# Last attention chunk: softmax reciprocals on turned sums and the output projection tile by tile; first eight MLP tiles transposed before the quantisation scale is known

## The chip, the cores and the metric

The kernel runs on one core of one Trainium2 chip. The metric is the device time of one execution in microseconds (us), as the median of several runs. TensorE is PE in the profile (PEld is its weight load), VectorE is DVE, ScalarE is ACT, GpSimd is POOL, SyncE, which issues most DMAs, is SP (SPq in rows on its queue).

## The reference, cut to what matters

```python
def reference(x, ctx_1024, g_xattn, g_ffn, Wq, bq, Wk, bk, Wv, bv, Wo, bo, w1, b1, w2, b2):
    # x: (2, 2048, 512), ctx_1024: (2, 77, 512), 16 heads of 32, hidden width 2048
    x = x + tanh(g_xattn[0]) * attention(layernorm(x), ctx_1024, ctx_1024, ...)   # softmax over 77 keys
    x = x + tanh(g_ffn[0]) * ffn(layernorm(x))
    return x

def _quant_per_tensor(x):
    scale = max(max(abs(x)), 1e-6) / 127.0        # one scale for the whole tensor
    return round(x / scale), scale

def ffn(x):
    h = qlinear(x, w1, b1)                        # quantised x and w1, product times both scales
    return qlinear(gelu(h, approximate=False), w2, b2)
```

The scale of the first quantised product needs the largest absolute value of the whole normalised tensor, so nothing can be rounded for the MLP before the last token of the attention is done.

## The kernel before, in words

The 4096 tokens are 8 chunks of 512 (`NC`), each 4 tiles of 128 (`TT`). PSUM has 8 banks of 128x512 f32. The program has three blocks with a barrier of all engines between them: `attention`, `hidden` (first MLP product and GELU) and `output` (second product). Each engine's instructions are written out by hand, and semaphores tie the engines together; there is no scheduler.

**attention**: a step for each chunk, in a pipeline two chunks deep. `values` and `sums` (L477, L487) multiply the exponentials with V and with a pattern of ones, so that bank `BS` holds the softmax sums: partition 32r+j holds the sum of head 4j+r for j below 4 (group j, place r), the token is the column. For a chunk, `reciprocals` (DVE, L937) inverts the whole bank of 128x512, and `divide` (DVE) does for each of four groups of heads a shuffle that spreads the group's rows over 32 partitions (L930) and a product (L932). `c_high` (ACT, L721) and `c_low` (POOL, L1174) split the result in two parts for a product of f32 precision in three terms, so that `project_out` (PE, L503) has 12 matmuls for each tile. `residual` (DVE, L944) adds to the residual stream `x1`; `stats2`/`tail_stats` and `tail_mean` (L951, L966, L973), ACT's centring (L727, L823) and `amax2`/`tail_amax` (L960, L978) give mean, variance and largest absolute value; POOL's `rstd_2` (L1154) gives the reciprocal standard deviation.

The last step (`last_steps` of every engine) does this for chunk 7, whose projection (L628) goes first through the head groups 0 and 1 for all four tiles and then tile by tile through groups 2 and 3. 36 idle transposes of the identity (`idle_turns`, L60) follow it on PE. Chunks 0 and 1 (tiles 0 to 7) have been normalised in place by POOL two steps earlier.

**hidden**: DVE reduces the maxima, PE turns them (L1437), DVE makes the scale (L1515 to L1520). Then tiles 0 to 7 are prepared: DVE scales each and adds a magic number that rounds (`y`, L1532), PE transposes the result (`magic_words`, L1394), ACT or DVE subtracts the magic number and writes bf16 into `xq_t` (L1467, L1525). `half` (L1405) is a half of one of the first three products of the first pair of chunks. Each `m` of a pair of chunks is 8 matmuls (L1421), a GELU on ACT (L1493) into a ring of four tiles `h_ring`, a maximum on DVE (L1582) and a DMA of 512 KB to memory on SP (L1355), which the GELU four places on waits for:

```python
                            act.wait_ge(h_out[m % RING], 16 * ((MF // RING) * j + m // RING))
```

Tiles from 8 on are normalised by DVE (`normalized`, `round_tile`, L1553 and L1562) beside the products. On SP the block begins with two loads on the same queue as all its stores:

```python
                sp.dma_start(w2_raw[:, :, :], w2_t.rearrange("(m p) d -> p m d", p=P)).then_inc(w2_in, 16)
                sp.dma_start(sh.b2[:], b2.rearrange("(o d) -> o d", o=1).to_broadcast([P, D])).then_inc(b2_in, 16)
```

Of the kernel before, what the change touches and what calls it, by code (L numbers as in the profile page):

```python
# [22 lines left out]
P = 128  # L23
# [103 lines left out]
def attention(nc, sem, sh, x, x_t, ctx_t, wq_t, wk_t, wv_t, wo_t, bq, bk, bv, bo, w1_t, b1, g_xattn, g_ffn,  # L127
# [8 lines left out]
    with ExitStack() as own:  # L136
# [46 lines left out]
        wq_mean = rsum_g  # L183

# [66 lines left out]
        rsum_on = sem("rsum_on")  # L251
        shuf_on = sem("shuf_on")
# [35 lines left out]
        def row_bank(n):  # L288

            return BS if n == 1 else BC  # L290

# [12 lines left out]
        with nc.Block() as block:  # L304
# [69 lines left out]
            def _(pe):  # L374
# [116 lines left out]

                def project_out(c, t, begin, end):
# [118 lines left out]
                def last_steps():  # L611
                    values(LAST, GROUPS - 1)
                    sums(LAST, GROUPS - 1)
                    project_out(LAST - 1, 1, 6, ALL)
                    pe.wait_ge(x1_on, TT * (LAST - 1) + 1)
                    project_out(LAST - 1, 2, 0, ALL)
                    pe.wait_ge(c_on, GROUPS * NC)
                    project_out(LAST - 1, 3, 0, ALL)

                    hi, lo = c_parts(LAST)  # L620
                    pe.wait_ge(exp_on, PAIRS * NC)
                    first_half = [(k, t) for k in range(KD // 2) for t in range(TT)]
                    second_half = [(k, t) for t in range(TT) for k in range(KD // 2, KD)]
                    for k, t in first_half + second_half:
                        if t == 0:
                            pe.wait_ge(c_lo_on, GROUPS * LAST + k + 1)
                        for a, w in ((hi, wo_hi), (hi, wo_lo), (lo, wo_hi)):
                            mm = nc.tensor.matmul(ps[:, t, :], a[:, k, t * P:(t + 1) * P], w[:, k, :],  # L628
                                                  start=(k == 0 and a is hi and w is wo_hi),
                                                  stop=(k == KD - 1 and a is lo))  # L630
                        if k == KD - 1:
                            mm.then_inc(o_mm, 1)
                    idle_turns(nc, sh, BS, 36)
# [17 lines left out]
            def _(act):  # L651
# [54 lines left out]
                def c_copy(c, g):  # L706
# [6 lines left out]
                    nc.scalar.copy(c_sb[:, g, :], ps[:, BC, :]).then_inc(c_on, 1)  # L713

# [128 lines left out]
            def _(dve):  # L843
# [230 lines left out]
                def last_steps():  # L1074
                    reciprocals(LAST)
                    divide(LAST, 0)
                    residual(LAST - 1, 1)
                    divide(LAST, 1)
                    divide(LAST, 2)
                    residual(LAST - 1, 2)  # L1080
                    divide(LAST, 3)
                    residual(LAST - 1, 3)
                    for t in range(1, TT):
                        stats2(LAST - 1, t)
                    for t in range(1, TT):
                        amax2(LAST - 1, t)
                    for t in range(TT + 3):
                        if t < TT:
                            residual(LAST, t)
                        if 0 <= t - 1 < TT:  # L1090
                            tail_stats(t - 1)
                        if 0 <= t - 2 < TT:
                            tail_mean(t - 2)
                        if 0 <= t - 3:
                            tail_amax(t - 3)
# [178 lines left out]
def hidden(nc, sem, sh, w2_t, b2):  # L1274
# [13 lines left out]
    with ExitStack() as own:  # L1288
# [27 lines left out]
        words_act = sem("words_act")  # L1316
        words_dve = sem("words_dve")
# [8 lines left out]
        T0, T1, TX, TW = 4, 5, 6, 7  # L1326
# [4 lines left out]
        WORD_BANKS = (T0, T1, 1, 3, TW)  # L1331
        BY_DVE = (1, 3, 6)

        def words_copied(u):

            by_dve = sum(v <= u for v in BY_DVE)
            return (words_dve, by_dve) if u in BY_DVE else (words_act, u + 1 - by_dve)

        def words(u):
            return ps[:, WORD_BANKS[u % len(WORD_BANKS)], :].rearrange("p (k n) -> p k n", k=KD)  # L1340

        def first_bank(m):

            return TX if m == 2 else 2 * (m % 2)

        with nc.Block() as block:
# [29 lines left out]
            def _(pe):  # L1376
                def transposes(n, u):

                    pe.wait_ge(xq_on, n - PT + 1)
                    if not isinstance(n, int) or n >= PT + 2:  # L1380
                        pe.wait_ge(xqt_on, n - PT - 1)
# [6 lines left out]
                def magic_words(u):  # L1388

                    pe.wait_ge(y_on, u + 1)  # L1390
                    if u >= len(WORD_BANKS):
                        pe.wait_ge(*words_copied(u - len(WORD_BANKS)))
                    for k in range(KD):
                        mm = nc.tensor.transpose(ps[:, WORD_BANKS[u % len(WORD_BANKS)], k * P:(k + 1) * P],  # L1394
                                                 y[:, u % YS, k * P:(k + 1) * P], sh.ident[:])
                    mm.then_inc(xqt_mm, 1)

                def half(m, s):

                    pe.wait_ge(words_act, (PT if s else TT) - sum(u < (PT if s else TT) for u in BY_DVE))  # L1400
# [436 lines left out]
```

## Time and profile before

| | |
|---|---|
| median of 3 runs | 607.31 us (606.14 to 607.54) |
| profiled execution | 604.76 us, span 603.0 us, mean granted clock 0.994 |
| PE busy | 578.5 us (96%) |
| DVE busy | 465.3 us (77%) |
| ACT busy | 335.3 us (56%) |
| POOL busy | 246.6 us (41%) |
| attention block / hidden / output | to 355.8 / 355.8 to 486.3 / from 486.3 us |

Times in rows are microseconds from the start of the span. In a timeline row the first number is the start, the second how long the piece took, `x4` how many instructions are merged in it, and the bracket how long the engine had been idle before it and who released it. Matmuls overlap in the pipeline, so that their pitch (start to start) is less than the duration of one. A row of windows gives the granted TensorE clock as a share of 2.4 GHz.

### The profile page before, as it was taken

Reading aid. Unit: us, or ns where it says so; the run is one execution under the profiler, and the core shown is the slowest. Engines: PE = TensorE matmul, PEld = TensorE weight load, DVE = VectorE, ACT = ScalarE, POOL = GpSimd, SP = SyncE. Lnnn points to the kernel's source line nnn. Section 1 sums busy time; section 2 is a strip of 40 time slices with the busy share of each in tenths; the row PEclk is TensorE's granted clock in tenths of the full one; section 3 lists DMA queues with packets and bytes.
Section 4 is the critical chain, followed back from the end, with each engine's and each line's share of the span. In section 5 each row is a group of like instructions: output and inputs, shape, how many; then the busy total and the mean of one; then the engine's idle time right before and its main releaser. Section 6 shows DMA issues by size and latency. Waiting matters only on the chain. (4 is left out here: it accounts for less than half of the span.)

```text
span 603.0 us, 9328 instructions
## 1 busy us (share of the span) xinstructions
PE 578.5 (96%) x3340; PEld 333.1 (55%) x3340; DVE 465.3 (77%) x667; ACT 335.3 (56%) x406; POOL 246.6 (41%) x211
## 2 busy tenths in 40 slices
PE   6999899999998999999999979999999999999997
PEld 5853656657466466585665765444444454444443
DVE  5865997868869779686796887989998689955281
ACT  1556273573753836628246326777776678544440
POOL 3368366464651664916072410000003619223383
PEclk8999999999999999999999989999999999999999
DMA  9926010320411404102001149777777967799766
GB/s 305 400 92 194 33 51 6 104 107 1 176 35 38 174 0 149 63 21 86 0 1 71 71 174 357 287 280 281 278 268 289 424 234 283 265 363 366 248 221 209
DMA packets 41223, 105.57 MB, mean 175 GB/s; under 512 B 3168, under 2 KB 3936, under 8 KB 36576
## 3 DMA queue, kind: packets, MB, share of 16 engines
q1 hardware_dynamic: 39840, 103.70, 46.7%
q10 hardware_dynamic: 1344, 1.37, 0.8%
q8 instruction: 23, 0.38, 0.2%
q14 instruction: 16, 0.13, 0.1%
HBM read 63.11 MB, written 41.94 MB: 174 GB/s over the span
## 5 line engine op out<-in xcount | busy, mean ns | idle before, releaser
L1421 PE MATMUL ps<-h_sb,w_q 128*128 (+1 forms) x488 | 109.6, 379 | 0.5 <-ACT xo L1493 0.5
L1714 PE MATMUL ps<-w_q,h_q 128*128 128x512 bf16 x448 | 96.9, 379 | 0.0
L1797 POOL TENSOR_TENSOR xo<-xo,b2s 128x512 f32<-128x512 f32 x32 | 52.7, 1680 | 69.1 <-DMA xo<-x_dram 51.0
L1421 PEld LDWEIGHTS ps<-h_sb,w_q 128*128 128x128 bf16 x488 | 46.6, 98 | 52.7 <-ACT xo L1493 1.1
L1714 PEld LDWEIGHTS ps<-w_q,h_q 128*128 128x128 bf16 x448 | 43.7, 98 | 53.0
L1493 ACT ACTIVATE xo<-ps,b1s,sc 128x1024 f32<-128x1024 f32 x48 | 57.6, 1204 | 21.1 <-PE ps L1421 17.7
L689 ACT ACTIVATE q_hi<-ps,bq_sb 128x512 fp32r<-128x512 f32 x32 | 22.0, 688 | 83.5 <-DVE ps L904 77.4
L703 ACT ACTIVATE prob<-ps 77x1024 f32<-77x1024 f32 x64 | 61.6, 1013 | 12.2 <-PE ps L464 12.2
L1582 DVE TENSOR_REDUCE hmax<-xo 128x1024 f32 (+1 forms) x48 | 57.0, 1212 | 4.4 <-ACT xo L1493 4.4
L1144 POOL TENSOR_TENSOR xt_lo<-xr,xt_hi 128x512 fp32r<-128x512 f32 x28 | 35.8, 1298 | 54.8 <-ACT xt_hi L682 54.6
L1774 DVE SCALAR_TENSOR_TENSOR xo<-ps,hs,xo 128x512 f32<-128x512 f32 x32 | 23.3, 746 | 39.9 <-POOL xo L1797 38.7
L420 PE MATMUL ps<-xt_hi,wq_hi 128*128 128x512 f32 x128 | 52.4, 410 | 0.7 <-POOL xt_lo L1144 0.7
L1174 POOL TENSOR_TENSOR c_lo<-c_sb,c_hi 128x512 fp32r<-128x512 f32 x28 | 38.8, 1407 | 32.0 <-ACT c_hi L721 32.0
L1611 POOL TENSOR_SCALAR h_sb<-h_sb,sc 128x2048 f32<-128x2048 f32 x4 | 7.9, 1974 | 104.9 <-DVE sc L1590 104.9
L420 PE MATMUL ps<-xt_lo,wq_hi 128*128 128x512 f32 x128 | 50.6, 395 | 0.0
L420 PE MATMUL ps<-xt_hi,wq_lo 128*128 128x512 f32 x128 | 50.5, 395 | 0.0
L922 DVE TENSOR_REDUCE neg_max<-ps 128x16 f32<-128x1232 f32 x32 | 45.9, 1434 | 4.5 <-PE ps L431 4.4
L503 PE MATMUL ps<-wo_hi,c_hi 128*128 128x512 f32 x112 | 47.0, 420 | 0.5 <-DVE q_lo L908 0.5
L503 PE MATMUL ps<-wo_hi,c_lo 128*128 128x512 f32 x112 | 44.8, 400 | 0.0
L503 PE MATMUL ps<-wo_lo,c_hi 128*128 128x512 f32 x112 | 44.2, 395 | 0.0
L960 DVE TENSOR_REDUCE amax<-cen 128x1 f32<-128x512 f32 x28 | 19.0, 678 | 29.5 <-ACT cen L727 29.5
L1191 POOL TENSOR_TENSOR x<-x,bo_gate 128x512 f32<-128x512 f32 x32 | 40.4, 1298 | 0.0
(174 smaller groups left out, 1119.1 us busy)
## 6 DMA issues: line engine op xcount, KB each, us to landing
h_dram<-xo SPq DMA_DIRECT2D x48, 512.0 KB, 2.7
h_sb<-h_dram SPq DMA_DIRECT2D x16, 1024.0 KB, 11.1
x_dram<-x SPq DMA_DIRECT2D x8, 1024.0 KB, 4.5
xo<-x_dram SPq DMA_DIRECT2D x8, 1024.0 KB, 4.8
x<-h_dram SPq DMA_DIRECT2D x8, 1024.0 KB, 7.9
x<-in_x SPq DMA_DIRECT2D x7, 1024.0 KB, 7.4
xr<-in_x_t SPq DMA_DIRECT2D x28, 256.0 KB, 3.0
out<-xo SPq DMA_DIRECT2D x7, 1024.0 KB, 8.3
```

Of the source, the lines that this page charges most:

```text
L420: mm = nc.tensor.matmul(ps[:, W0 if m % 2 == 0 else W1, :], w[:, k, m * P:(m + 1) * P], r[:, k, :], start=(j == 0), stop=(j == len(terms) ...
L503: mm = nc.tensor.matmul(ps[:, bank, :], a[:, k, t * P:(t + 1) * P], w[:, k, :], start=(j == 0), stop=(j == len(terms) - 1))
L703: nc.scalar.activation(prob[0:NK, p % SLOTS, :].rearrange("p (s n) -> p s n", s=2), ps[0:NK, 2 * (p % 2):2 * (p % 2) + 2, :], ACT.Exp).the ...
L922: nc.vector.tensor_reduce(neg_max[:, :, :].rearrange("p t (r j) -> p t r j", j=DK)[:, :, :, m], ps[:, 0:TT, 0:4 * NK].rearrange("p t (h n) ...
L1144: nc.gpsimd.tensor_tensor(xt_lo[:, k, :], xr[:, k % 2, :], xt_hi[:, k, :].bitcast(F32), ALU.subtract).then_inc(xt_lo_on, 1)
L1174: nc.gpsimd.tensor_tensor(lo[:, g, :], c_sb[:, g, :], hi[:, g, :].bitcast(F32), ALU.subtract).then_inc(c_lo_on, 1)
L1191: nc.gpsimd.tensor_tensor(xa, xa, sh.bo_gate[:], ALU.add).then_inc(xg_on, 1)
L1421: mm = nc.tensor.matmul(ps[:, 2 * (m % 2) + s, :], w1_q[:, k, m * P:(m + 1) * P], xq_t[:, one(2 * j + s), k, :], start=(k == 0), stop=(k = ...
L1493: nc.scalar.activation(dst.rearrange("p (s n) -> p s n", s=2), ps[:, bank:bank + 2, :], ACT.Gelu, bias=b1s[:, m:m + 1], scale=sc[:, 4:5]). ...
L1582: nc.vector.tensor_reduce(dst, src, AX.X, ALU.max, apply_absolute_value=True).then_inc(hmax_on, 1)
L1714: mm = nc.tensor.matmul(ps[:, 4 * s + t, :], h_q[s][:, m, t * P:(t + 1) * P], w2_q[:, m, :], start=(m == 0), stop=(m == MF - 1))
L1797: nc.gpsimd.tensor_tensor(xo[:, s, t, :], xo[:, s, t, :], b2s[:], ALU.add).then_inc(xb_on, 1)
```

## The change

It has two parts.

**Last chunk of the attention.** ACT copies the sums out of PSUM, PE transposes them (`turn_sums`), so that the token is the partition and a reciprocal of 128x64 elements does (`last_reciprocals`). ACT spreads one group's reciprocals over 32 columns each (`widen_reciprocals`), PE transposes that back into PSUM (`spread_reciprocals`), and DVE multiplies from there (`last_divide`), without a shuffle. These stand inside the projection of chunk 6. Chunk 7's projection goes tile by tile through all four groups. DVE's order of residuals and statistics is new. The Gelu table load stands behind the four `c_high`.

**Start of the MLP.** The first eight normalised tiles are transposed in f32 before the scale is known: seven at the end of the attention block, in the place of the 36 idle transposes, and the eighth in `hidden`. ACT (six tiles) and DVE (two) scale them out of PSUM into `y`, DVE subtracts the magic number and writes bf16 (`rounded`). The banks of the first products, the place of bank `TX`, and the waits for the bank of tile 8 are adapted.

```diff
@@ attention, PE
+                def turn_sums():
+                    pe.wait_ge(last_sums_on, 1)
+                    for t in range(TT):
+                        mm = nc.tensor.transpose(ps[:, GROUPS - 1, t * P:(t + 1) * P], rsum[:, t * P:(t + 1) * P],
+                                                 sh.ident[:])
+                    mm.then_inc(last_sums_mm, 1)
+                def spread_reciprocals(g):
+                    pe.wait_ge(last_wide_on, g + 1)
+                    for t in range(TT):
+                        mm = nc.tensor.transpose(ps[:, g, t * P:(t + 1) * P], rec_wide(g)[:, t * P:(t + 1) * P],
+                                                 sh.ident[:])
+                    mm.then_inc(last_row_mm, 1)
...
                     project_out(LAST - 1, 1, 6, ALL)
+                    turn_sums()
                     pe.wait_ge(x1_on, TT * (LAST - 1) + 1)
-                    project_out(LAST - 1, 2, 0, ALL)
+                    project_out(LAST - 1, 2, 0, 3)
+                    for g in range(GROUPS):
+                        spread_reciprocals(g)
+                    project_out(LAST - 1, 2, 3, ALL)
                     pe.wait_ge(c_on, GROUPS * NC)
                     project_out(LAST - 1, 3, 0, ALL)
...
-                    idle_turns(nc, sh, BS, 36)
+                    for t in range(TT):
+                        project_out(LAST, t, 0, ALL)
+                    pe.wait_ge(normal_on, 2 * (TT + 1))
+                    pe.wait_ge(x1_on, TT * LAST)
+                    pe.wait_ge(last_sums_on, 1)
+                    for u in range(2 * TT - 1):
+                        if u >= TT:
+                            pe.wait_ge(x1_on, TT * LAST + u - TT + 1)
+                        for k in range(KD):
+                            nc.tensor.transpose(ps[:, (u + TT) % 8, k * P:(k + 1) * P], x1[:, u, k * P:(k + 1) * P],
+                                                sh.ident[:])
@@ attention, ACT
+                def widen_reciprocals(g):
+                    act.wait_ge(last_rec_on, 1)
+                    if g == 0:
+                        act.wait_ge(last_sums_mm, 1)
+                    elif g >= 2:
+                        act.wait_ge(last_row_mm, g - 1)
+                    nc.scalar.copy(rec_wide(g).rearrange("p (t r j) -> p t r j", t=TT, r=4),
+                                   rec_t[:, :, :, g:g + 1].to_broadcast([P, TT, 4, DK])).then_inc(last_wide_on, 1)
...
                     c_copy(LAST, GROUPS - 1)
-                    nc.scalar.activation(bk_sb[:, 0:1], sh.bq[:, 0:1], ACT.Gelu)
+                    act.wait_ge(sum_mm, GROUPS * NC)
+                    act.wait_ge(shuf_on, GROUPS * LAST)
+                    nc.scalar.copy(rsum[:], ps[:, BS, :]).then_inc(last_sums_on, 1)
+                    for g in range(GROUPS):
+                        widen_reciprocals(g)
                     for g in range(GROUPS):
                         c_high(LAST, g)
+                    nc.scalar.activation(bk_sb[:, 0:1], sh.bq[:, 0:1], ACT.Gelu)
@@ attention, DVE
+                def last_reciprocals():
+                    dve.wait_ge(last_sums_mm, 1)
+                    turned = ps[:, GROUPS - 1, :].rearrange("p (t r j) -> p t r j", t=TT, r=4)
+                    nc.vector.reciprocal(rec_t, turned[:, :, :, 0:GROUPS]).then_inc(last_rec_on, 1)
+                def last_divide(g):
+                    dve.wait_ge(c_on, GROUPS * LAST + g + 1)
+                    dve.wait_ge(last_row_mm, g + 1)
+                    nc.vector.tensor_tensor(c_sb[:, g, :], c_sb[:, g, :], ps[:, g, :], ALU.mult).then_inc(cn_on, 1)
@@ hidden, PE
-                idle_turns(nc, sh, TW, 12)
-                for u in range(TT):
-                    magic_words(u)
-                half(0, 0)
-                magic_words(4)
-                magic_words(5)
-                half(1, 0)
-                magic_words(6)
-                magic_words(7)
-                half(2, 0)
+                pe.wait_ge(xmax_on, 3)
+                for k in range(KD):
+                    mm = nc.tensor.transpose(turned(PT - 1)[:, k * P:(k + 1) * P], x1[:, PT - 1, k * P:(k + 1) * P],
+                                             sh.ident[:])
+                mm.then_inc(turned_last, 1)
+                pe.wait_ge(*scaled_value(0))
+                idle_turns(nc, sh, T0, 8)
+                for m in range(3):
+                    half(m, 0)
                 for m in range(3):
                     half(m, 1)
@@ hidden, ACT
+                act.wait_ge(xs_on, 2)
                 for u in range(PT):
                     if u not in BY_DVE:
-                        transposed(0, u)
+                        if u >= YS:
+                            act.wait_ge(words_on, rounded_value(u - YS))
+                        if u == PT - 1:
+                            act.wait_ge(turned_last, 1)
+                        nc.scalar.activation(y[:, u % YS, :], turned(u), ACT.Copy, bias=MAGIC,
+                                             scale=sc[:, 3:4]).then_inc(scaled_act, 1)
@@ hidden, DVE
+                scaled(2)
+                for u in (0, 2, 1, 3):
+                    rounded(u)
+                scaled(5)
+                for u in (4, 5, 6):
+                    rounded(u)
```

PE's order between the last softmax sums and the block's end. First before (the L503 rows are chunk 6's tiles 1 to 3, L628 is chunk 7; rows that repeat are left out at "..."), then with the change (L506 `turn_sums`, L514 `spread_reciprocals`, L529 projection, L658 the tiles turned ahead):

```order
L487 MATMUL ps<-prob,ones_g 32x512 x4
L503 MATMUL ps<-wo_hi,c_hi 128x512
...
L628 MATMUL ps<-wo_hi,xt_lo 128x512
...
L60 MATMUL ps<-ident 128x128 x36
```

```order
L506 MATMUL ps<-ident,rsum 128x128 [waits last_sums_on]
L506 MATMUL ps<-ident,rsum 128x128 x3
L529 MATMUL ps<-wo_hi,c_hi 128x512 [waits x1_on]
L529 MATMUL ps<-wo_lo,c_hi 128x512
L529 MATMUL ps<-wo_hi,c_lo 128x512
L514 MATMUL ps<-ident,rsum 128x128 [waits last_wide_on]
...
L514 MATMUL ps<-ident,row 128x128 [waits last_wide_on]
...
L529 MATMUL ps<-wo_hi,xt_hi 128x512 [waits c_hi_on]
...
L658 MATMUL ps<-ident,x 128x128 [waits last_sums_on,x1_on,normal_on]
```

Twenty transposes and five waits now stand inside chunk 6's projection, ahead of all of chunk 7's, and 28 real transposes stand where the idle ones stood.

DVE's end of the attention block, before (L937 reciprocal, L930 and L932 shuffle and product, L944 residual, L951 and L955 statistics, L960 maximum) and with the change (L984 reciprocal, L989 products, L996 residual, L1018 and L1025 statistics, L1030 maximum):

```order
L937 RECIPROCAL rsum<-ps 128x512 [waits cn_on,sum_mm]
L930 STREAM_SHUFFLE rsum_g<-rsum 128x512 [waits cn_on,rsum_on,c_on]
L932 TENSOR_TENSOR c_sb<-c_sb,rsum_g 128x512 [waits shuf_on]
L944 SCALAR_TENSOR_TENSOR x<-ps,gate,x 128x512 [waits xg_on,o_mm]
...
L960 TENSOR_REDUCE amax<-cen 128x1 [waits ln2_cen] x3
L944 SCALAR_TENSOR_TENSOR x<-ps,gate,x 128x512 [waits xg_on,o_mm] x2
L966 BN_STATS st<-x 128x6 [waits x1_on]
```

```order
L996 SCALAR_TENSOR_TENSOR x<-ps,gate,x 128x512 [waits xg_on,o_mm]
L984 RECIPROCAL rsum_g<-ps 128x64 [waits last_sums_mm]
L1003 BN_STATS st<-x 128x6 [waits x1_on]
L1007 BN_AGGR mv<-st 128x2 [waits ln2_stats]
L989 TENSOR_TENSOR c_sb<-c_sb,ps 128x512 [waits last_row_mm,c_on] x4
...
L996 SCALAR_TENSOR_TENSOR x<-ps,gate,x 128x512 [waits xg_on,o_mm]
L1018 BN_STATS st<-x 128x6 [waits x1_on]
L1025 BN_AGGR mv<-st 128x2 [waits ln2_stats]
L1030 TENSOR_REDUCE amax<-c_sb 128x1 [waits tail_cen] x2
```

The four shuffles are gone, chunk 6's statistics are spread between its residuals, and behind the last residual stand one tile's statistics and two maxima.

## Rows read from the trace of the kernel before

**Rows 1.** PE-bound loops: the page's costliest groups; line, shape, count, busy us and mean ns, idle before.

```profile
L1421 PE MATMUL ps<-h_sb,w_q 128*128 (+1 forms) x488 | 109.6, 379 | 0.5 <-ACT xo L1493 0.5
L1714 PE MATMUL ps<-w_q,h_q 128*128 128x512 bf16 x448 | 96.9, 379 | 0.0
```

**Rows 2.** Timeline of PE, end of the attention block.

```profile
328.02 0.50 PE L503 MATMUL ps<-wo_hi,c_hi 128*128 128x512 f32 x1
...
342.87 0.50 PE L628 MATMUL ps<-wo_hi,xt_hi 128*128 128x512 f32 x1 [1.07 <-POOL xt_lo L1174]
...
347.65 0.39 PE L628 MATMUL ps<-wo_hi,xt_lo 128*128 128x512 f32 x1
347.88 2.34 PE L60 MATMUL ps<-ident 128*128 128x128 f32 x20
```

**Rows 3.** Timeline of DVE, the last chunk's reciprocals.

```profile
328.15 3.36 DVE L937 RECIPROCAL rsum<-ps 128x512 f32<-128x512 f32 x1 [2.10 <-PE ps L487]
```

**Rows 4.** Timeline of ACT, first split of the last chunk.

```profile
333.13 0.62 ACT L721 CAST xt_hi<-c_sb 128x512 fp32r<-128x512 f32 x1 [3.74 <-DVE c_sb L932]
```

**Rows 5.** Timeline of POOL, same stretch.

```profile
333.83 1.29 POOL L1174 TENSOR_TENSOR xt_lo<-c_sb,xt_hi 128x512 fp32r<-128x512 f32 x1 [13.25 <-ACT xt_hi L721]
```

**Rows 6.** Timeline of DVE, end of attention and start of hidden.

```profile
350.70 0.72 DVE L944 SCALAR_TENSOR_TENSOR x<-ps,gate,x 128x512 f32<-128x512 f32 x1
...
352.58 0.68 DVE L966 BATCH_NORM_STATS2 st<-x 128x6 f32<-128x512 f32 x1
...
353.84 0.17 DVE L973 BATCH_NORM_AGGREGATE mv<-st 128x2 f32<-128x6 f32 x1
354.14 1.35 DVE L978 TENSOR_REDUCE amax<-c_sb 128x1 f32<-128x512 f32 x2
...
357.66 0.16 DVE L1520 RECIPROCAL sc<-sc 128x1 f32<-128x1 f32 x1
...
360.42 0.69 DVE L1525 TENSOR_SCALAR h_sb<-ps 128x512 bf16<-128x512 f32 x1 [0.89 <-PE ps L1394]
```

**Rows 7.** Timeline of POOL, the last reciprocal deviation.

```profile
354.37 1.01 POOL L1154 TENSOR_TENSOR rstd<-ve,minus_half 128x4 f32<-128x4 f32 x1
```

**Rows 8.** Timeline of PE, start of hidden.

```profile
355.81 1.08 PE L60 MATMUL ps<-ident 128*128 128x128 f32 x4 [3.84 <-PEq L304]
...
362.13 1.02 PE L1405 MATMUL ps<-h_sb,w_q 128*128 128x512 bf16 x4 [0.88 <-DVE h_sb L1525]
...
365.60 3.62 PE L1405 MATMUL ps<-h_sb,w_q 128*128 128x512 bf16 x16
```

**Rows 9.** Timeline of PE, products m=5 and m=6 of the first pair.

```profile
373.62 3.62 PE L1421 MATMUL ps<-h_sb,w_q 128*128 128x512 bf16 x16
```

**Rows 10.** Timeline of ACT, the first three GELUs.

```profile
367.58 3.40 ACT L1493 ACTIVATE xo<-ps,b1s,sc 128x1024 f32<-128x1024 f32 x3 [1.18 <-PE ps L1405]
```

**Rows 11.** Groups of 355.7 to 372, shapes apart: a rounding from SBUF to bf16.

```profile
L1562 DVE TENSOR_SCALAR xq<-y 128x512 bf16<-128x512 f32 x2 | 0.9, 426 | 0.2
```

**Rows 12.** Windows; columns: us, busy and count by engine, granted clock, DMA share, GB/s.

```profile
352.00:353.00 1.00, 0.00 (x0) 0.00 (x0) 1.00 (x4) 0.72 (x1) 0.00 (x0) 1.00 0.90 377
356.00:357.00 1.00, 1.00 (x6) 1.00 (x6) 0.19 (x2) 0.00 (x0) 0.29 (x1) 0.50 0.11 31
```

**Rows 13.** SP's queue, the loads of w2 and b2 and the first store.

```profile
356.24 3.75 SPq L1350 DMA_DIRECT2D b_sb<-in_b  x1
369.01 30.69 SPq L1355 DMA_DIRECT2D h_dram<-xo  x18
```

**Rows 14.** DMA issues of 16 to 20 us, KB each, us to landing.

```profile
x<-in_w_t SPq DMA_DIRECT2D x1, 4096.0 KB, 18.5
...
b_sb<-in_b SPq DMA_DIRECT2D x1, 8.0 KB, 18.2
```

**Rows 15.** The same of 354 to 357 us (b2).

```profile
b_sb<-in_b SPq DMA_DIRECT2D x1, 256.0 KB, 14.0
```

**Rows 16.** The same of 367 to 370 us (first store).

```profile
h_dram<-xo SPq DMA_DIRECT2D x1, 512.0 KB, 3.7
```

More of the change, by code:

```diff
@@ L290, in row_bank, with rec_wide @@
             return BS if n == 1 else BC
+        def rec_wide(g):
+            return rsum if g % 2 == 0 else row
         def rstd_value(c):
@@ L1074, in last_steps @@
                 def last_steps():
-                    reciprocals(LAST)
-                    divide(LAST, 0)
                     residual(LAST - 1, 1)
-                    divide(LAST, 1)
-                    divide(LAST, 2)
+                    last_reciprocals()
+                    stats2(LAST - 1, 1)
+                    for g in range(GROUPS):
+                        last_divide(g)
                     residual(LAST - 1, 2)
-                    divide(LAST, 3)
+                    stats2(LAST - 1, 2)
+                    amax2(LAST - 1, 1)
                     residual(LAST - 1, 3)
[L1083 to L1095, printed above, removed]
+                    stats2(LAST - 1, 3)
+                    amax2(LAST - 1, 2)
+                    amax2(LAST - 1, 3)
+                    for t in range(TT):
+                        residual(LAST, t)
+                        tail_stats(t)
+                        tail_mean(t)
+                        if t:
+                            tail_amax(t - 1)
+                    tail_amax(TT - 1)
                 nc.vector.memset(v[64:P, :, :], 0.0).then_inc(v_padded, 1)
@@ L1325, in hidden, with turned, scaled_value, rounded_value @@
         w2_done = sem("w2_done")
-        T0, T1, TX, TW = 4, 5, 6, 7
+        T0, T1, TX, TW = 4, 5, 3, 7
         def one(j):
             return j if isinstance(j, int) else bass.ds(j, 1)
[L1331 to L1340, printed above, removed]
+        BY_DVE = (2, 5)
+        ROUNDED = (0, 2, 1, 3, 4, 5, 6, 7)
+        def turned(u):
+            return ps[:, (u + TT) % 8, :]
+        def scaled_value(u):
+            return (scaled_dve, BY_DVE.index(u) + 1) if u in BY_DVE else (scaled_act, u + 1 - sum(v < u for v in BY_DVE))
+        def rounded_value(u):
+            return ROUNDED.index(u) + 1
         def first_bank(m):
-            return TX if m == 2 else 2 * (m % 2)
+            return (4, 6, 0)[m] if m < 3 else 2 * (m % 2)
         with nc.Block() as block:
@@ L1379, in transposes @@
                     pe.wait_ge(xq_on, n - PT + 1)
+                    if isinstance(n, int) and n == PT:
+                        pe.wait_ge(ident_b_on, 1)
+                        pe.wait_ge(h_on, 1)
                     if not isinstance(n, int) or n >= PT + 2:
@@ L1386, in transposes @@
                     mm.then_inc(xqt_mm, 1)
[L1388 to L1396, printed above, removed]
                 def half(m, s):
-                    pe.wait_ge(words_act, (PT if s else TT) - sum(u < (PT if s else TT) for u in BY_DVE))
-                    pe.wait_ge(words_dve, sum(u < (PT if s else TT) for u in BY_DVE))
-                    if m == 2:
-                        pe.wait_ge(xmax_on, 3)
+                    pe.wait_ge(words_on, PT if s else TT)
+                    if m == 2 and s == 0:
+                        pe.wait_ge(*scaled_value(TT))
                     for k in range(KD):
@@ L1413, in step @@
                     for m in range(3 if first else 0, MF):
-                        if first and m == 4:
-                            pe.wait_ge(h_on, 1)
-                        else:
+                        if not first or m > 3:
                             pe.wait_ge(h_on, MF * j + m - 1)
```

65 lines of the change are left out of this document (27 added, 38 removed).

## The prediction

> **What bounds the kernel now.** I read the page first: PE is busy 96% of the span. The costliest groups then show where a saving counts: the loops of both MLP products have next to no idle time ahead of their matmuls [rows 1], so from the seventh product of the first pair of chunks to the end PE works without a gap, and whatever time that point is reached earlier the end is earlier too. The change works only on the stretch in front of it, from 328 to 375 us, and the timelines show what sets the pace there. PE is dense until 347.9 us with one gap of 1.07 us for POOL's low parts [rows 2]; then DVE and POOL alone finish the statistics, PE idles 3.84 us, and the `hidden` block begins at 355.81 [rows 6 to 8]. There the granted clock is 0.50, 1.2 GHz, where it was 1.00 before the pause [rows 12]. The first real product starts at 362.13, the first GELU at 367.58 [rows 8, 10]. The point to compare is the start of product m=6: eight matmuls into the piece of [rows 9], 373.62 + 1.73 = 375.35 us.
>
> **End of the attention block.** The 78 projection matmuls from 328.02 on are the same before and after, so only what lies between them is costed.
> - Added on PE: 4 + 16 transposes at the pitch of the idle turns, 2.34 / 20 = 0.117 us [rows 2]: +2.34.
> - Added wait for the first widened group. PE has done six matmuls (0.233 us apart) by 329.4 and the four turned sums by 330.1. DVE has the residual of tile 1 in front (0.72 us [rows 6]), to 330.4. A reciprocal of 512 elements costs 3.36 us [rows 3] and of one 0.16 [rows 6], so 6.3 ns each: 64 cost 0.55, to 330.95. ACT's widening copy is shown nowhere; the cast of the same size costs 0.62 [rows 4], the end is 331.65. PE, with three matmuls in between, has been free since 330.6: +1.05.
> - Added hand-offs for groups 1 to 3: each copy takes 0.15 longer than four transposes, and the third also waits until its buffer has been read: +0.6 in all.
> - Removed: the gap of 1.07 and the slow start behind it, and a short one ahead of chunk 7: -1.2. It goes because chunk 7's low parts (four times 0.62 on ACT, then 1.29 on POOL [rows 4, 5]) are ready by 339.5, and the last of them is first needed near 341.6. The 3.36 us reciprocal and four shuffles leave DVE.
>
> So PE's last projection matmul moves from 347.65 to 350.45: **later** by 2.8 us. What follows it is shorter. Before, DVE came to chunk 7's residuals late and ran the last one at 350.70 and the last mean at 353.84, behind other tiles' work [rows 6]. Now, with 2.8 us between tiles, three are finished when the fourth arrives: residual from 350.9 (0.72), statistics 0.68, mean 0.17 give 352.5. POOL needs 1.37 from that mean to its last result (354.01 to 355.38 [rows 6, 7]): 353.85. The two maxima fit beside it. PE's 28 transposes (3.3 us) end at about 354.1. The block ended 0.3 us after the last of these before, so `hidden` starts at 354.2, **1.6 us earlier**. The removed idle turns were hidden; the new transposes run in the time that they and the pause took. The Gelu table load moves behind the four splits, ahead of centrings that are 10 us from mattering.
>
> **Start of the MLP.** The scale was ready 2.0 us after the block began (357.82 against 355.81 [rows 6, 8]), part of it behind four turns at the lower clock. With PE busy to the end I take 1.5: 355.7. Then DVE scales a tile out of PSUM (0.69, as [rows 6]) beside ACT, and rounds four from SBUF at 0.43 each [rows 11]: 358.15. ACT's three tiles at 0.6 are in time. The first product starts there rather than at 362.13. For the second halves DVE needs 0.69 + 4 x 0.43 and some 0.65 of small operations: 361.3. The twelve first-half matmuls (0.216 apart) end at 360.8, so PE waits 0.5. Before, the second halves began after four matmuls of the piece at 365.60, at 366.46 [rows 8]. So this point and the first GELU come 5.15 us earlier, the latter at 362.4. Tile 8 waits for the first GELU, which is done by then.
>
> **What gives some of it back.** Each of the four ring tiles is free for the GELU four places on only when its 512 KB are in memory. SP's queue holds w2 (4 MB) and b2 in front of the first store. In the trace an 8 KB load queued behind 4 MB took 18.2 us, landing with it (18.5 [rows 14]); so a store does not pass what is ahead of it. Before, b2 landed at 356.24 + 14.0 = 370.24, and the first store, issued at 369.01, hardly met it [rows 13, 15, 16]. Now both loads move by the block's 1.6 us only, to 368.65, while the store is issued at 363.8 and must wait. Its own transfer: 4352 KB took 14.0 us, so 512 KB take 1.65; the first store before landed 2.5 after b2 (369.01 + 3.7). I take 1.65, since now the queue never runs dry: 370.3. The GELU of m=4, which could start near 368, ends at 371.5, and m=6, which needs its banks, starts at 371.55. That is 375.35 - 371.55 = **3.8 us gained**; with 2.5 it is 3.0. The next stores land 1.2 to 1.7 us apart, no slower than PE makes tiles (1.73), so I price them at nothing; if this cover is gone it costs some tenths each.
>
> The profiled execution would go from 604.76 to 601.0. It lies 2.55 below the median of the runs; from the median the same 3.8 give **603.5 us**.
>
> **The rivals.**
> - *The store passes the loads* or lands early. Then m=6 is at 375.35 less 5.15 and a little of the 0.5 wait ahead of m=3, gain 5.3: 602.0. [Rows 14] speaks against it. 0.18.
> - *The attention block ends no earlier*: hand-offs of PE, ACT and DVE cost more than the tenths that I gave them, or the last products are slowed by POOL beside them. The loads then start at 355.8 and the gain is 2.2: 605.1. 0.13.
> - *The clock falls in the prelude.* PE fell to 1.2 GHz after the 3.84 us pause; now its longest pause is under 1 us, but it is only about half busy from 354 to 358. The twelve first-half matmuls would take twice 2.6 us. The second halves then start near 363.4 and the GELU of m=4 near 370.6, where the store holds it to 370.3 anyway: 603.8. 0.10. The Trainium skill (TensorE: Matmul & The Clock Gate, on the second failure mode of the clock) says that frequent short pauses between groups of matmuls can make the clock swing between its levels. By that rule this rival would happen; the trace has no such prelude to show it, and its 1.00 through the other short waits of PE speaks against.
> - *Slower*: the widening copies. Each reads one element 32 times over, and PE waits for all four with nothing to cover it. If reading so costs e more than 0.62, the block ends 4e later. From e = 1.4 (a copy of 2.0 us) the kernel is slower than before by over 0.3%; at four times 0.62 it is 7.5 - 3.8 = 3.7 slower: 611.0. The broadcast weights of PE's turns cost nothing extra, which says little of ACT. 0.05.
> - *No difference* (within 1.8 us), by several small losses together: 0.04.
>
> **How the numbers follow.** The forecast case has 0.50. A measurement of this kernel tells a difference of about 0.3%, 1.8 us, from none. Faster: 0.50 + 0.18 + 0.10 and most of the 0.13, with a part lost to noise, 0.88. Same: the rest of the second rival and the last, 0.07. Slower 0.05. The range takes the first two rivals, the two prices of the store (603.5 and 604.3) and 0.7 us of spread between runs: 601.4 to 605.4.
>
> **What would show it.** The profile after should have: the reciprocal of 128x64 at 0.5 to 0.6 us; widening copies of about 0.6; the last projection matmul 2 to 3 us later than before, yet `hidden` starting at about 354.2; clock 1.00 across the boundary; the first GELU near 362.4; then an idle time of ACT of about 2 us before the GELU of m=4 put down to the DMA of `h_dram`, and PE idle 1 to 2 us before m=6; nothing else changed behind it. The prediction is wrong if the widening copies are long, if ACT does not wait for the first store, or if the stretch from m=6 to the end is not as long as before.

## The result, and the profile after

The changed kernel takes 603.55 us (median of 13 runs, 600.1 to 605.95), the kernel before, run beside it, 606.24 (13 runs, 603.0 to 608.01). The ratio is 0.9954 with a 95% interval of 0.9935 to 0.9973: 2.8 us less, 1.6 to 3.9. The forecast was 603.5 from a median of 607.31, so a gain of 3.8. The median of the kernel before came out 1.1 us lower over more runs, which makes the hit on 603.5 partly luck; the gain is what there is to explain.

| | before | after |
|---|---|---|
| profiled execution, span | 604.76, 603.0 us | 603.55, 601.8 us |
| last softmax sums to the start of `hidden` | 28.79 | 27.14 |
| `hidden` | 130.52 | 129.97 |
| `output`, to the end of the last result | 114.16 | 114.99 |
| PE busy, mean clock | 578.5 us, 0.994 | 577.0 us, 0.994 |

The three lengths are taken the same way for every kernel below: from the start of PE's last piece of `sums` (327.02 and 327.18 us) to the first idle turn of `hidden` (355.81, 354.32), from there to the first idle turn of `output` (486.33, 484.29), and to the end of DVE's last result (600.49, 599.28). They leave out what differs from one execution to the next ahead of the change. In sum the change saves 1.65 + 0.55 - 0.83 = 1.4 us in the profiles.

The end of the attention block on PE, by its timeline (line numbers are those of the changed kernel: L514 brings the reciprocals back, L658 turns the seven tiles, L1452 the first half products, L1466 the loop), answering to [rows 2, 8, 9]:

```profile
331.81 0.66 PE L514 MATMUL ps<-ident,rsum 128*128 128x128 f32 x4 [0.82 <-ACT rsum L748]
...
333.51 0.65 PE L514 MATMUL ps<-ident,rsum 128*128 128x128 f32 x4 [0.52 <-ACT rsum L748]
...
350.62 3.22 PE L658 MATMUL ps<-ident,x 128*128 128x128 f32 x28
354.32 0.63 PE L60 MATMUL ps<-ident 128*128 128x128 f32 x4 [0.48 <-PEq L314]
...
358.23 5.35 PE L1452 MATMUL ps<-h_sb,w_q 128*128 128x512 bf16 x24 [0.53 <-DVE h_sb L1578]
...
367.36 1.89 PE L1466 MATMUL ps<-h_sb,w_q 128*128 128x512 bf16 x8
371.87 2.38 PE L1466 MATMUL ps<-h_sb,w_q 128*128 128x512 bf16 x8 [2.63 <-ACT xo L1533]
374.05 0.63 PE L1442 MATMUL ps<-ident_b,xq 128*128 128x128 bf16 x4
```

The same on DVE, against [rows 3, 6]: the reciprocal, the last residual, the last maximum:

```profile
330.55 0.55 DVE L984 RECIPROCAL rsum_g<-ps 128x64 f32<-128x64 f32 x1
...
350.82 0.75 DVE L996 SCALAR_TENSOR_TENSOR x<-ps,gate,x 128x512 f32<-128x512 f32 x1 [0.53 <-PE ps L529]
...
353.30 0.69 DVE L1030 TENSOR_REDUCE amax<-c_sb 128x1 f32<-128x512 f32 x1 [0.22 <-ACT c_sb L864]
```

And on ACT, against [rows 4, 10]: a widening copy, and the GELUs of m=0 to 2, 3 and 4:

```profile
331.14 0.62 ACT L748 COPY rsum<-rsum_g 128x512 f32<-128x512 f32 x1 [2.24 <-DVE rsum_g L984]
...
361.94 3.40 ACT L1533 ACTIVATE xo<-ps,b1s,sc 128x1024 f32<-128x1024 f32 x3 [2.50 <-issue]
...
365.69 1.23 ACT L1533 ACTIVATE xo<-ps,b1s,sc 128x1024 f32<-128x1024 f32 x1
370.61 1.20 ACT L1533 ACTIVATE xo<-ps,b1s,sc 128x1024 f32<-128x1024 f32 x1 [3.69 <-issue]
```

The reciprocals cost 0.55 us where 3.36 stood. PE pays for it with twenty transposes and two pauses (0.82 and 0.52), and its last projection matmul starts later (350.39 against 347.65), yet `hidden` starts 1.5 us earlier. The first GELU is 5.6 us earlier. Then ACT stands still for 3.69 us before the GELU of m=4, and PE for 2.63 us before m=6. The profile names no releaser for ACT's wait ("issue"); what ties it to the store is the time: the first store, issued at 363.38, took 7.2 us to land, at 370.6, and the GELU starts at 370.61.

```profile
h_dram<-xo SPq DMA_DIRECT2D x1, 512.0 KB, 7.2
```

The next thing is the clock. Windows of one us (busy time and count of PE, PEld, DVE, ACT, POOL; granted clock; DMA share; GB/s):

```profile
370.00:371.00 1.00, 0.00 (x0) 0.00 (x0) 0.00 (x0) 0.39 (x1) 0.00 (x0) 1.00 1.07 406
...
372.00:373.00 1.00, 1.00 (x6) 0.43 (x5) 1.00 (x1) 0.61 (x2) 0.00 (x0) 1.00 0.99 383
373.00:374.00 1.00, 1.00 (x4) 0.36 (x3) 0.15 (x2) 0.88 (x1) 0.00 (x0) 0.58 1.03 397
374.00:375.00 1.00, 1.00 (x7) 0.67 (x6) 1.00 (x1) 0.71 (x1) 0.00 (x0) 0.50 0.46 174
...
376.00:377.00 1.00, 1.00 (x4) 0.34 (x3) 1.00 (x2) 0.00 (x0) 0.00 (x0) 0.72 0.79 301
377.00:378.00 1.00, 1.00 (x6) 0.49 (x5) 0.25 (x1) 0.56 (x1) 0.00 (x0) 1.00 0.98 375
```

Behind the pause the clock fell to 0.50, 1.2 GHz, a little after work had begun again, for over 3 us. The transposes behind m=6 start at 374.05, 3.0 us earlier than before (377.07), those behind m=8 at 378.97, only 1.8 us earlier (380.75). The last stretch, DVE and PE:

```profile
598.53 0.75 DVE L1825 SCALAR_TENSOR_TENSOR xo<-ps,hs,xo 128x512 f32<-128x512 f32 x1 [0.47 <-POOL xo L1848]
```

```profile
500.80 96.86 PE L1765 MATMUL ps<-w_q,h_q 128*128 128x512 bf16 x448
```

PE ends at 597.66, 2.05 us earlier than before, but the last result now waits for POOL's addition, which waits for a load of `x1`; before, it followed PE at once. POOL's last four additions, before and after:

```profile
593.96 4.94 POOL L1797 TENSOR_TENSOR xo<-xo,b2s 128x512 f32<-128x512 f32 x4 [7.33 <-DMA xo<-x_dram]
```

```profile
593.49 4.94 POOL L1848 TENSOR_TENSOR xo<-xo,b2s 128x512 f32<-128x512 f32 x4 [7.03 <-DMA xo<-x_dram]
```

Counted from the block's start they begin at 107.6 us before the change and at 109.2 us with it.

### The profile page after: what moved, and what is told of

It reads as the page before. It is cut to its first block and busy times, and to the rows that moved or that the text cites. A ratio compares the mean times of both kernels' runs of the same rounds, so it can differ in the third digit from the quotient of the medians.

```text
span 601.8 us, 9279 instructions
## 1 busy us (share of the span) xinstructions
PE 577.0 (96%) x3320; PEld 329.7 (55%) x3320; DVE 457.9 (76%) x658; ACT 338.7 (56%) x412; POOL 246.5 (41%) x211
## 3 DMA queue, kind: packets, MB, share of 16 engines
q10 hardware_dynamic: 1344, 1.37, 0.8%
## 5 line engine op out<-in xcount | busy, mean ns | idle before, releaser
L1466 PE MATMUL ps<-h_sb,w_q 128*128 (+1 forms) x488 | 111.3, 383 | 2.7 <-ACT xo L1533 2.6
L1466 PEld LDWEIGHTS ps<-h_sb,w_q 128*128 128x128 bf16 x488 | 46.9, 99 | 55.8 <-ACT xo L1533 3.9
L529 PE MATMUL ps<-wo_hi,c_hi 128*128 128x512 f32 x112 | 47.2, 421 | 0.5 <-DVE q_lo L949 0.5
L529 PE MATMUL ps<-wo_hi,c_lo 128*128 128x512 f32 x112 | 44.9, 401 | 0.0
L529 PE MATMUL ps<-wo_lo,c_hi 128*128 128x512 f32 x112 | 44.2, 394 | 0.0
L1797 ACT ACTIVATE h_q<-h_sb 128x2048 bf16<-128x2048 f32 x16 | 29.7, 1904 | 21.2 <-DVE h_sb L1818 11.3
```

The lines of the kernel that those rows point to most:

```text
L529: mm = nc.tensor.matmul(ps[:, bank, :], a[:, k, t * P:(t + 1) * P], w[:, k, :], start=(j == 0), stop=(j == len(terms) - 1))
L1466: mm = nc.tensor.matmul(ps[:, 2 * (m % 2) + s, :], w1_q[:, k, m * P:(m + 1) * P], xq_t[:, one(2 * j + s), k, :], start=(k == 0), stop=(k = ...
L1797: nc.scalar.activation(h_q[u % 2][:, q * MQ:(q + 1) * MQ, :], h_piece(u // 2, u % 2, q), ACT.Copy, bias=-MAGIC).then_inc(hq_on, 1)
```

## The experiments

Nine further kernels and three repeats (e11, e13, e14), beside the change and the kernel before. All lengths are those defined above, from one profile each.

| kernel | ratio to before (95%) | attention's end | hidden | output |
|---|---|---|---|---|
| before | | 28.79 | 130.52 | 114.16 |
| before again (e14) | | 28.77 | 130.62 | 114.16 |
| before, w2 in pieces (e12) | 1.0019 (0.9991 to 1.0046) | 28.76 | 130.44 | 114.16 |
| the change | 0.9954 (0.9935 to 0.9973) | 27.14 | 129.97 | 114.99 |
| the change again (e11) | 0.9953 (0.9927 to 0.9979) | 27.14 | 129.70 | 115.16 |
| attention part alone (e3) | 0.9914 (0.9882 to 0.9946) | 27.13 | 129.54 | 114.17 |
| attention part alone, again (e13) | 0.9943 (0.9920 to 0.9966) | 27.13 | 129.62 | 114.17 |
| MLP part alone (e4) | 0.9953 (0.9930 to 0.9977) | 28.78 | 127.77 | 115.29 |
| change, w2 from ScalarE (e1) | 0.9937 (0.9913 to 0.9961) | 27.14 | 129.85 | 114.43 |
| change, turns in the stall (e6) | 0.9927 (0.9899 to 0.9955) | 27.13 | 128.32 | 115.98 |
| change, w2 in pieces (e7) | 0.9887 (0.9854 to 0.9919) | 27.13 | 125.40 | 114.95 |
| change, output order (e8) | 0.9932 (0.9905 to 0.9959) | 27.14 | 129.56 | 114.16 |
| change, both of these (e9) | 0.9887 (0.9855 to 0.9920) | 27.13 | 125.41 | 114.16 |
| attention part, output order (e10) | 0.9946 (0.9924 to 0.9969) | 27.14 | 129.40 | 114.16 |

**e1: w2 on another queue.**

```diff
-                sp.dma_start(w2_raw[:, :, :], w2_t.rearrange("(m p) d -> p m d", p=P)).then_inc(w2_in, 16)
+                nc.scalar.dma_start(w2_raw[:, :, :], w2_t.rearrange("(m p) d -> p m d", p=P)).then_inc(w2_in, 16)
```

> The changed kernel with the 4 MB load of w2 issued by ScalarE, on its own queue, and nothing but b2 ahead of the first store on SP's queue. Theory (the store waits its turn behind w2): the first store lands within 5 us of its issue instead of 7.2, ScalarE's idle time of 3.7 us before the GELU of m=4 shrinks to under 1.5, product m=6 starts near 370.0 instead of 371.87, the clock stays at 1.00 through 373 to 377, and the output block begins near 481 instead of 484.3. Rival (memory or the DMA engines are simply full, whichever queue): the store lands as late as before and nothing moves. For the end, two theories: if PE sets it, the span falls by the same 3 us, to about 598.5; if the transfers of the output block set it, by 1 us at most.

```profile
372.72 1.20 ACT L1532 ACTIVATE xo<-ps,b1s,sc 128x1024 f32<-128x1024 f32 x1 [3.54 <-issue]
```

```profile
h_sb<-in_w_t ACTq DMA_DIRECT2D x1, 4096.0 KB, 19.5
...
b_sb<-in_b SPq DMA_DIRECT2D x1, 256.0 KB, 4.5
```

My theory fell. The first store takes 7.0 us to land (7.2 in the change), the GELU of m=4 starts 16.12 us after the block does (16.29), PE pauses 2.47, and the clock falls as well. b2 now lands in 4.5 us (14.5 in the change) and w2 takes 19.5 (14.3), so what stands in SP's queue does move beside w2 and w2 ends later; but the store is not served first. Whose queue the 4 MB stand in makes no difference of use; e7 below tests whether their being under way at all does. How the engines divide their time between the queues, this run does not tell.

**e3 and e4: each part alone.** For e3 the hidden block of the kernel before follows the new end of the attention, with 28 idle turns in the place of the 28 transposes:

```diff
-                    for u in range(2 * TT - 1):
...
+                    idle_turns(nc, sh, BS, 28)
```

> Only the attention part; the MLP starts as before, and 28 idle turns stand where the change turns seven tiles. Theory: hidden starts at 354.3 as in the changed kernel, the clock is 1.00 there, so the scale is ready 0.5 us sooner after the block's start and the turns ahead of the first products are not at half rate; first GELU 2.3 to 3 us before 367.58. The first store is issued at about 366 and meets b2's landing at 368.7, so ScalarE waits under 1 us for it; output block at 484 (2 to 2.5 before 486.3). Rival (the gain needs the earlier turned tiles): 1.6 us, output block at 484.7.

```profile
354.08 0.63 PE L60 MATMUL ps<-ident 128*128 128x128 f32 x4 [0.48 <-PEq L314]
...
359.16 1.02 PE L1450 MATMUL ps<-h_sb,w_q 128*128 128x512 bf16 x4 [0.88 <-DVE h_sb L1570]
```

```profile
371.37 1.20 ACT L1538 ACTIVATE xo<-ps,b1s,sc 128x1024 f32<-128x1024 f32 x1 [1.26 <-DMA h_dram<-xo]
```

It saves 1.66 us at the attention's end, as in the whole change, and another 0.9 to 1.0 in `hidden`. The first GELU comes 10.53 us after the block's start against 11.77 before, because the clock never fell: the four idle turns take 0.63 us against 1.08 in [rows 8], and twelve more 1.47 against 2.60. ACT waits 1.26 us for the first store, where I had expected under 1. In the profiles it beats or equals the whole change in every block.

For e4 the MLP part follows the attention's old end:

```diff
-                    idle_turns(nc, sh, BS, 36)
+                    pe.wait_ge(normal_on, 2 * (TT + 1))
+                    pe.wait_ge(x1_on, TT * LAST)
+                    pe.wait_ge(rsum_on, NC)
+                    for u in range(2 * TT - 1):
...
```

> Only the MLP part; the attention's end is that of the kernel before, but the tiles are turned where the idle turns stood. Theory: hidden starts at 355.8 with the clock at 0.50, since PE has again paused over 3 us; first GELU near 364.5 (3 earlier); the loads of w2 and b2 land as before near 370.2, so the GELU of m=4 waits for the first store until about 372; product m=6 near 373.4, after a PE pause of 2 us or more, with the clock falling behind it; output block 485 to 486, so under 1.3 us gained. Rival (no wait for the store): output block at 483.

```profile
355.98 0.82 PE L60 MATMUL ps<-ident 128*128 128x128 f32 x4 [4.73 <-PEq L304]
...
360.27 6.75 PE L1410 MATMUL ps<-h_sb,w_q 128*128 128x512 bf16 x24
...
373.06 1.90 PE L1424 MATMUL ps<-h_sb,w_q 128*128 128x512 bf16 x8 [0.38 <-ACT xo L1491]
```

PE pauses 4.73 us before `hidden`, the clock is down in the prelude (24 half products in 6.75 us against 5.35 in the change), so the point where the store is due comes later, and PE waits only 0.38 us at m=6: product m=6 at 373.06, where I had 373.4. What I had wrong is the pause, put at 2 us or more, and that the clock would fall behind it. It stayed up, and `hidden` is 2.75 us shorter, twice what I had allowed. So **in `hidden` alone each part gains, 0.9 and 2.75 us, and both together 0.55 to 0.8**: the earlier the first store is issued, the longer it waits behind w2, and with both parts the clock falls behind the wait.

**e6: turns in the stall.**

```diff
+                        if first and m == 6:
+                            idle_turns(nc, sh, TW, 20)
```

> The changed kernel with 20 idle transposes (2.3 us) ahead of product m=6, where PE waits 2.63 us. Theory (the pause lowers the clock, and that costs 1.7 us after the stall): m=6 starts at 371.9 as before, the clock stays at 1.00 from 373 to 377, the transposes after m=8 start at 377.3 instead of 378.97, and the output block begins 1.7 us sooner, at 482.6. Rival (the loss behind the stall is a backlog of ScalarE and VectorE): nothing moves. The end falls by 1.7 if PE sets it, by less than 0.6 if the output block's transfers do.

```profile
371.31 2.35 PE L60 MATMUL ps<-ident 128*128 128x128 f32 x20
374.04 1.90 PE L1468 MATMUL ps<-h_sb,w_q 128*128 128x512 bf16 x8 [0.38 <-ACT xo L1535]
...
376.12 3.63 PE L1468 MATMUL ps<-h_sb,w_q 128*128 128x512 bf16 x16
```

```profile
375.00:377.00 2.00, 2.00 (x14) 0.93 (x13) 1.14 (x2) 1.95 (x2) 0.00 (x0) 1.00 0.87 334
377.00:379.00 2.00, 2.00 (x11) 0.93 (x10) 1.89 (x4) 1.74 (x3) 0.00 (x0) 1.00 0.94 356
```

Product m=6 starts 17.48 us after the block does, as in the change (17.55), the clock stays at 1.00, and `hidden` takes 128.32 instead of 129.97: 1.65 us, as expected to a tenth. From the start of m=6 to the output block it takes 110.84 us, the kernel before 110.98 (486.33 - 375.35), and the four profiles in which the clock fell there (the change, e1, e8, e11) 112.27 to 112.47. So the fall costs 1.4 to 1.6 us, and without it nothing is left of the loss behind the stall. Its output block was the longest of all, 115.98, so that only 0.67 us of it reached the end in the profile, and the timed runs (0.9927 against 0.9954) don't set the two kernels apart.

**e7: w2 in pieces.** With the queue ruled out, the bytes ahead of the first store were cut:

```diff
-                sp.dma_start(w2_raw[:, :, :], w2_t.rearrange("(m p) d -> p m d", p=P)).then_inc(w2_in, 16)
+                load_w2(0, 10)
...
+                for m in range(MF):
+                    store_h(0, m)
+                    if 5 <= m < 11:
+                        load_w2(m + 5, m + 6)
```

> The changed kernel with only 10 of w2's 16 row blocks (2.5 MB) loaded ahead of the first store, and the other six one by one behind the stores of m=5 to 10. On another queue the load held the store up as long as on the same one, so what counts now is how many bytes are ahead in the DMA engines, not whose queue they are in. Theory: the first 2.5 MB are through 9 us after the block begins, when the first store is issued; the GELU of m=4 waits for it under 1 us (3.7 before), product m=6 starts 15.5 to 16 us after the block's start instead of 17.55, the clock stays at 1.00, and the hidden block takes 126.5 to 127 us instead of 129.9. Rival (the store is slow by itself while GELUs and products run): the wait stays over 2 us.

```profile
h_sb<-in_w_t SPq DMA_DIRECT2D x1, 2560.0 KB, 10.3
...
h_dram<-xo SPq DMA_DIRECT2D x1, 512.0 KB, 3.3
b_sb<-in_b SPq DMA_DIRECT2D x1, 256.0 KB, 10.5
```

w2's first part lands 10.3 us after its issue, the first store 3.3 us after its own, and ACT no longer waits for it: the GELU of m=4 starts 13.0 us after the block does instead of 16.3. `hidden` takes 125.40, better than the 126.5 I expected, since the wait is gone altogether. Against the kernel before that is 5.1 us: 4.15 of it are there at the first GELU (7.62 us after the block's start against 11.77), 4.8 at that of m=4 (13.0 against 17.8). With the attention's 1.65 the two parts are worth 6.8 us up to the output block without the store's wait, where I had worked out 5.3.

**e12: the control.**

> The kernel before with w2 in pieces: the control. Theory (the load of w2 costs something only when the first store comes before it is through): hidden block within 0.5 us of 130.5. Rival (spreading w2 helps by itself, whatever comes before): hidden block under 129.5.

130.44 against 130.52 and 130.62: w2 in pieces gives nothing where nothing comes early. The measured ratio agrees. With e1 and e7 this shows that what the store waits for is the bytes under way, not its place in a queue.

**e8, e9, e10: the output block.**

```diff
-                load_h(3, 0)
                 store(0, 1)
                 load_x1(1, 1)
+                load_h(3, 0)
+                store(1, 0)
+                load_x1(2, 0)
                 load_h(3, 1)
```

> The changed kernel with the stores of chunks' results and the loads of x1 that follow them put ahead of the loads of h in the output block. In the changed kernel the last results wait for GpSimd, which waits for x1, though TensorE is done 0.9 us earlier. Theory (the chain of store, load of x1 and GpSimd sets the end, since it stands behind 1 MB loads of h that nobody needs yet): the last result follows TensorE's last matmul at once, the output block takes 114.2 us as in the kernel before instead of 115.0, so 0.8 us less. Rival (the engines' bandwidth, not the order, sets that chain): the last addition of GpSimd stays 109 us after the block's start.

> Both of the foregoing: w2 in pieces and the new order in the output block. If both theories hold, hidden takes 126.5 to 127 us and output 114.2, so the span falls by 3.5 to 4 us below that of the changed kernel, and the ratio to the kernel before is near 0.988. If either stays what it was, the trace shows which.

> The attention part alone with the new order in the output block. The attention part alone ended with TensorE setting the pace, so a new order has nothing to give there: output block 114.2 us as without it, hidden block 129.5. If it is faster in the output block than 114.1, the order does something else than I think. Its ratio to the kernel before should be that of the attention part alone, 0.991; if it comes out near 0.995 the difference seen between that part alone and the whole change was noise of the runs.

The end of e9 on DVE:

```profile
591.39 0.75 DVE L1840 SCALAR_TENSOR_TENSOR xo<-ps,hs,xo 128x512 f32<-128x512 f32 x1 [2.70 <-PE ps L1780]
```

In e8 and e9 the output block is back at 114.16, with PE as the last releaser and POOL's last piece starting 105.7 and 105.5 us after the block's start instead of 109.2. In e10 the order gives nothing, as expected, since PE set the end there without it. So in the profiles the order is worth 0.8 us. The ratios don't show it: e7 and e9 have the same, and e8's differs from the change's by less than either interval. But every timed run has its span and granted clock on record, and at a like clock e9's runs are the shorter ones: 598.7 and 598.9 us at 0.991 against e7's 599.2 and 599.8, 594.7 at 1.000 against 595.7, and 0.4 to 1.0 us less in each of the six pairs. So the longer output block is there in the timed runs too, though six runs of each are few. With w2 in pieces the kernel is 1.1% faster than before (e9: 0.8 to 1.45%), more than twice what the change gives. By the lengths that is 5.4 us below the change, where I had expected 3.5 to 4.

**e11, e13, e14: the same kernels again.**

> The changed kernel, unaltered, beside the next runs on one chip. In every profile of a kernel with the MLP part the output block took 114.4 to 116.0 us, in the two without it 114.2. If the change itself causes that, this profile shows over 114.4 again, with GpSimd's last addition over 108.6 us after the block's start; if it is chance from run to run, it can be anything from 114.16 up. Hidden block 129.5 to 130.0, attention's end 27.1.

> The attention part alone once more, beside the whole change. By the blocks of the profiles it should be level with the whole change to within 1.3 us: attention's end 27.1, hidden 129.5, output 114.2. Ratio to the whole change 0.996 to 1.000; if it comes out above, the MLP part gives something on top that the profiles don't show.

> The kernel before, unaltered, for one more profile of its output block. If 114.2 there is the kernel's own, it is 114.2 again, with GpSimd's last addition 107 to 108 us after the block's start; if it comes out over 114.4, the longer output blocks of the changed kernels are chance.

The lengths of all blocks repeat, the output block's too: 114.16 to 114.17 in all five profiles without the MLP part and with the old order, 114.4 to 116.0 in all six with it. So the longer output block belongs to the MLP part. PE ends 113.4 us after the block's start in all fourteen profiles; what is longer is the chain that ends in POOL's last addition. It first falls behind at the second store of results: issued 36 us into the block, it took 19.2 to 19.7 us to land in the five, and 20.6 to 21.6 us in the six. Why it does, no run shows: the code of that block is the same. The attention part alone is level with the whole change in the timed runs of e13 (0.9943 against 0.9953), and ahead by 1.1 to 1.3 us in the profiles; the MLP part gives nothing on top of it as it stands. The 0.9914 of e3 is no better kernel: none of its six runs had a clock under 0.997, while those of e13 go down to 0.991.

## Why the prediction was right, and where it was not

- **Reciprocals, copies, hand-offs**: right. 0.55 for the reciprocal (0.55 worked out), 0.61 and 0.62 for the copies, so the slower rival had no footing. PE's wait for the first copy was 0.82 (1.05), for the third 0.52. The last projection matmul started at 350.39, where I had 350.45.
- **Attention's end**: 1.6 forecast, 1.5 on the clock of the profile, 1.65 by length. Right, with its mechanism: DVE is through three of the four tiles when the last projection ends.
- **Prelude**: `hidden` at 354.32 (354.2), the scale at 355.84 (355.7), the first product at 358.23 (358.15), the first GELU at 361.94 (362.4). The clock stayed at 1.00 through the pauses there, so that rival did not happen. Nor did the swing of the clock that the Trainium skill (TensorE: Matmul & The Clock Gate, on the second failure mode) tells of, in this place.
- **The store behind the loads**: the landing was put at 370.3 and came at 370.6; m=6 at 371.55, came at 371.87. The gain at this point was 3.5 against 3.8. The waits were longer than I had said (3.69 for "about 2" on ACT, 2.63 for "1 to 2" on PE), since the work ahead of them was done sooner. The size was right, the reason only in part: I said that a store does not pass what is ahead of it in SP's queue. e1 shows that it gains nothing from a queue of its own; e7 shows that it gains all when fewer bytes are under way.
- **"Nothing else changed behind it"**: wrong. This is the step that failed. I had priced PE's pause at its length only. It cost 1.4 to 1.6 us more, since the clock fell behind it (e6). I had weighed the clock in the prelude, where the pauses are short, and not at the stall that I had forecast myself just before.
- **"Whatever time that point is reached earlier the end is earlier too"**: wrong by 0.8 us. The page shows PE without idle time in the last loop, but [rows 1] don't show that POOL's last addition, at 598.90, ended only 0.8 us ahead of PE, at 599.71. With the MLP part, the chain of store, load and addition comes last.
- **The sum**: by the lengths the change gains 1.65 + 1.99 = 3.64 us up to m=6, where 3.8 was forecast. It loses 1.44 from there to the output block (112.42 against 110.98) and 0.83 in that block, which leaves 1.37 in the profile. The timed runs say 2.8 (1.6 to 3.9), and e11 the same again (1.3 to 4.4). Their interval just reaches the forecast's 3.8, and their middle lies some 1.4 us above the profiles. So two terms of 1.4 and 0.8 us were left out, and the small miss in the timed result is in part luck.
- **The gap between the two**: the granted clocks on record explain it in part. Half the clock for over 3 us takes some 0.003 off the mean of a 602 us span. One of the change's 13 runs and two of e11's 12 had 0.999, so in these the clock fell nowhere for so long, not behind the stall either; their spans are 598.3 to 598.8 us. None of the 64 runs of the kernel before whose clock is on record had more than 0.997, and the shortest span among them is 601.2. Between these the change gains 2.4 to 2.9 us, about the profile's 1.4 and the fall's 1.4 to 1.6 together. How many executions go without the fall the record does not tell, so how much of the gap it closes stays open.

## What to carry to other kernels

A head start is only worth as much as the next shared resource allows: ask what the earlier work will meet there, and count bytes under way, not queues. A pause of TensorE is priced at its length plus what the clock may lose behind it; here 20 idle turns inside the pause took the second part away in the profile. Two parts that each gain may gain less together than the better one, so time them apart.

## What the runs showed of the hardware that I had not expected

The clock also falls, or does not, in the same place of the same program. At 72 to 75 us, a stretch that no kernel here changes, PE has two pauses, of 1.22 and 1.54 us. In the change's first profile, by its timeline and window:

```profile
74.32 0.66 PE L455 MATMUL ps<-ident,neg_max 128*128 128x128 f32 x4 [1.53 <-DVE neg_max L963]
```

```profile
74.00:75.00 1.00, 0.68 (x8) 0.52 (x12) 0.97 (x4) 0.00 (x0) 0.79 (x1) 1.00 0.35 119
```

and in its second (e11):

```profile
74.38 1.12 PE L455 MATMUL ps<-ident,neg_max 128*128 128x128 f32 x4 [1.54 <-DVE neg_max L963]
```

```profile
74.00:75.00 1.00, 0.62 (x3) 0.62 (x4) 0.98 (x3) 0.00 (x0) 0.85 (x1) 0.50 0.30 92
...
78.00:80.00 2.00, 2.00 (x12) 2.00 (x11) 1.78 (x5) 2.00 (x4) 0.03 (x1) 0.50 0.00 0
```

There it is 0.50 for at least 5 us, and the last softmax sums start at 329.46 us instead of 327.18, 2.3 later. In every profile with 0.50 from 74 to 76 us (e1, e6, e7, e8, e11) they start at 329.3 to 329.5, in those with 1.00 at 327.0 to 327.3. In e10 the clock was low for a part of that stretch (0.56 from 74 to 76, 0.58 from 76 to 78), and they start at 328.1. e9 and e12 had the clock at 1.00 in the first 20 us, where the others had it at 0.57 to 0.73 from 11 to 15 us, and reached the same sums at 325.4. These two places, about 2 us each, are together more than the whole change gains. With the fall behind the stall they fit the spread of 5 to 6 us among runs of one kernel. Profiles of single executions must therefore be compared by the length of a stretch, not by when it ends.
